# A second MLP layer with stationary weights in a fused convolution and windowed-attention kernel, and one convolution matmul moved forward

## The chip, the core and the metric

The kernel runs as one program on one core of a Trainium2 chip. The metric is device time in microseconds (us), the median of several runs; lower is better. The core has five instruction streams that run side by side and meet at semaphores: TensorE (PE, matmuls; its weight loads are shown as PEld), VectorE (DVE), ScalarE (ACT), GpSimd (POOL) and SyncE (SP), which here issues all the DMAs. A strip of the work passes between them many times, so what counts is the longest chain through all of them.

## The reference

The input x is 32 images of 56 x 56 pixels with 128 channels, float32. Two layers follow each other.

```python
# layer 0: ResNeXt block (convolutions without bias, _bn = affine with fixed statistics)
h = relu(_bn(conv1x1(x, w1), ...))             # 128 -> 64 channels
h = relu(_bn(conv3x3(h, w2, groups=32), ...))  # 64 -> 64
h = _bn(conv1x1(h, w3), ...)                   # 64 -> 128
x = relu(h + x)
# layer 1: shifted-window attention block, windows of 7 x 7, 8 heads of 16
y   = roll(_ln(x, norm1_w, norm1_b), (-3, -3))
q, k, v = windows(y) @ qkv_w.T
attn = softmax(q @ k.T * scale + bias + mask)
x = x + roll(windows_back(attn @ v @ proj_w.T + proj_b), (3, 3))
z = _ln(x, norm2_w, norm2_b)
z = gelu(z @ fc1_w.T + fc1_b) @ fc2_w.T + fc2_b   # 128 -> 512 -> 128
return x + z
```

The change touches `@ fc2_w.T`, the second MLP layer, and the order of work in layer 0.

## The kernel before

There are two stages, one behind the other. All matmuls are float32.

**The convolution stage** goes over 16 pairs of images, the loop body holding two pairs and the last pairs being written out. An image pair is cut into 8 chunks of 7 rows. A pair is done in two steps of four chunks (`STEPS` = 2, `GROUPS` = 4). In a step, PE does conv2, the 3 x 3 convolution (line 517, 144 matmuls into banks 0 to 3), and conv3 in two halves of 32 matmuls (line 530), one for each image of the pair, again into banks 0 to 3. Between these, it already makes conv1 (line 497) for four chunks of the next pair: `x_to_channels` (line 488) turns a chunk of x so that channels lie on partitions, DVE copies it into the tile xct (`xct_out`, line 918), conv1 multiplies, and ACT writes the result to the tile h1 (`h1_out`, line 748). There is one xct buffer for each of the two images. `conv1(gp, i)` needs the copy of chunk i; `x_to_channels` for chunk i+1 comes right behind it in the function `produce`. The second half of conv3 may write the banks only when DVE has added the first half's results to x (`sum_out`, line 931). conv2 of the next step waits for the sums of the second half; conv2 of the next pair also waits for all eight h1 chunks. ACT finishes a chunk with a relu (`relu_out`, line 764), and SP stores it. Each engine runs its own list in the order in which its function `period` writes it; nothing is reordered across engines but by semaphores. On DVE the order in a step is: copies of chunks 1 and 2, the four sums of half 0, the copy of chunk 3, the four sums of half 1, the copy of the next chunk 0.

**The attention stage** goes over 256 strips, eight per image, each strip a row of 8 windows (392 pixels, `ST`), held as 4 pairs of windows of 98 pixels (`PAIRS`, `PT`). It is software-pipelined over strips: in one turn of `strips(t)`, PE does queries, keys, values and scores of strip t, the attention of strip t-1, and the MLP of strip t-3. DVE makes the layer norms, adds the bias to the scores and takes the maxima; POOL subtracts them; ACT does the exponentials, the Gelu and the copies out of PSUM. The order on each engine is again that of its `strips` function. The MLP of a strip uses one PSUM bank, `RC`, by turns (`C_JOBS` = 4 turns: z transposed, two of the four hidden chunks, the output), with the semaphores c_full and c_out; the other two hidden chunks go through bank `RA`. `mlp_out(t, p)` makes the MLP's output with pixels on partitions: for window pair p, four matmuls (line 659), one for each 128 hidden channels. The stationary operand is the 98-pixel piece of g, the moving one is fc2, 128 columns wide. That is 16 matmuls for each strip; two pairs stand ahead of `attend(t1, 1)` and two behind the transposes of the next strip's xn. DVE then adds the residual (`y_sum`, line 1039), and SP stores.

Other lines that the steps name: 582 `project` (queries, then keys), 567 transposes of xn and z, 575 values, 651 hidden layer, 592 scores, 605 transposes of the probabilities, 628 row sums, 617 `attend`, 638 output projection; on ACT 793 `xt_out`, 798 `q_out`, 823 `pt_out`, 829 and 832 `reciprocals`, 860 the load of the table for exponentials, 837 the exponentials; on DVE 1012 the norms, 1000 `ot_out` (the attention output times the reciprocal, which the projection reads).

Of the kernel before, what the change touches and what calls it, by code (L numbers as in the profile page):

```python
# [142 lines left out]
def program(nc, a, out):  # L143
# [6 lines left out]
    with ctx:  # L150
        def sb(name, shape, dtype=fp32):
            return ctx.enter_context(nc.sbuf_tensor(name, shape, dtype))
# [77 lines left out]
        z = sb("z", [PT, PAIRS, C])  # L230
        zt = sb("zt", [C, ST])
        g = sb("g", [128, HC, ST])
        y = sb("y", [PT, 2, PAIRS, C])

        bank = [ctx.enter_context(nc.psum_tensor(f"bank{i}", [128, 512], fp32)) for i in range(8)]
# [3 lines left out]
        B_JOBS = (4, 5)  # L239
        SUMS, PROJECTION = 3, 4  # L240
        SMALL = 6
        C_JOBS = 4


        conv_load, bias_load, wload, prep, tb_store, tb_load = sem("conv_load"), sem("bias_load"), sem("wload"), sem("prep"), sem("tb_store"), sem("tb_load")
# [218 lines left out]
        def _(pe):  # L464
# [33 lines left out]
                                          start=True, stop=True)  # L498
                mm.then_inc(conv1_ps, 1)

            def produce(gp, u, i):
                conv1(gp, i)
                if i + 1 < CHUNKS:
                    x_to_channels(gp, u, i + 1)
                elif later(gp, 1):
                    x_to_channels(gp + 1, 1 - u, 0)

            def conv2(gp, u, s):
                pe.wait_ge(h1_sb, CHUNKS * (gp + 1))
# [36 lines left out]
            def period(gp, u):  # L546
                for s in range(STEPS):
                    conv2(gp, u, s)
                    if later(gp, 1):
                        produce(gp + 1, 1 - u, GROUPS * s)  # L550
                        produce(gp + 1, 1 - u, GROUPS * s + 1)
                    conv3(gp, s, 0)
                    if later(gp, 1):
                        produce(gp + 1, 1 - u, GROUPS * s + 2)
                    conv3(gp, s, 1)
                    if later(gp, 1):
                        produce(gp + 1, 1 - u, GROUPS * s + 3)

            over_pairs(pe, fill, period)
            pe.wait_ge(prep, len(PREP))  # L560
# [90 lines left out]
                nc.tensor.matmul(ring[:, 0:ST], fc1[:, 128 * j:128 * j + 128], zt[:],  # L651
                                 start=True, stop=True).then_inc(full, 1)

            def mlp_out(t, p):

                pe.wait_ge(c_out, C_JOBS * t.n + 3)
                pe.wait_ge(hidden_out, 2 * t.n + 2)
                for c in range(HC):
                    mm = nc.tensor.matmul(RC[0:PT, C * p:C * p + C], g[:, c, PT * p:PT * p + PT], fc2[:, c, :],  # L659
                                          start=c == 0, stop=c == HC - 1)  # L660
                if p == PAIRS - 1:
                    mm.then_inc(c_full, 1)

            def strips(t):
                ahead, t1, t2, t3 = t.back(-1), t.back(1), t.back(2), t.back(3)
                if t.there():
                    pe.wait_ge(a_out, A_JOBS * t.n + 1)
                    project(t, 0)
                if t3.there():
                    pe.wait_ge(z_sb, t3.n + 1)  # L670
                    wait(pe, c_out, C_JOBS * t3.n)
                    to_channels(RC, z, c_full)
                if t.there():
                    values(t, 0)
                    project(t, 1)
                    values(t, 1)
                if t3.there():
                    hidden(t3, 0)
                if t.there():
                    scores(t, 0)  # L680
                if t3.there():
                    hidden(t3, 1)
                if t.there():
                    scores(t, 1)
                if t3.there():
                    hidden(t3, 2)
                if t1.there():
                    probs_t(t1, 0)
                    probs_t(t1, 1)
                if t3.there():  # L690
                    hidden(t3, 3)
                if t1.there():
                    probs_t(t1, 2)
                    probs_t(t1, 3)
                if t1.there():
                    row_sums(t1)
                    attend(t1, 0)
                if t3.there():
                    mlp_out(t3, 0)
                    mlp_out(t3, 1)  # L700
                if t1.there():
                    attend(t1, 1)
                if ahead.there():
                    pe.wait_ge(xn_sb, ahead.n + 1)
                    wait(pe, a_out, A_JOBS * ahead.n)
                    if t3.there():
                        pe.wait_ge(hidden_out, 2 * t3.n + 2)
                    to_channels(RA, xn, a_full)
                if t3.there():
                    mlp_out(t3, 2)  # L710
                    mlp_out(t3, 3)
                if t1.there():
                    projection(t1)

# [3 lines left out]
        def _(act):  # L718
# [54 lines left out]
            def period(gp, u):  # L773
                for s in range(STEPS):
                    h2_out(gp, s)
                    if later(gp, 1):
                        h1_out(gp + 1, 1 - u, GROUPS * s)
                        h1_out(gp + 1, 1 - u, GROUPS * s + 1)
                    relu_out(gp, u, s, 0)
                    if later(gp, 1):  # L780
                        h1_out(gp + 1, 1 - u, GROUPS * s + 2)
                    relu_out(gp, u, s, 1)
                    if later(gp, 1):
                        h1_out(gp + 1, 1 - u, GROUPS * s + 3)

            over_pairs(act, fill, period)
            for c in range(CHUNKS):
# [25 lines left out]
            def gelu(t, j):  # L813
                ring, full, out_, n = ((RC, c_full, c_out, C_JOBS * t.n + 2 + j // 2) if j % 2 == 0 else
                                       (RA, hidden_full, hidden_out, 2 * t.n + 1 + j // 2))
                act.wait_ge(full, n)
                nc.scalar.activation(g[:, j], ring[:, 0:ST], ACT.Gelu, bias=fc1b[:, j:j + 1]).then_inc(out_, 1)  # L817

            def pt_out(t, j):
                act.wait_ge(b_full[j % 2], b_before(t, j % 2, 1 + j // 2) + 1)  # L820
# [18 lines left out]
            def strips(t):  # L839
                ahead, t1, t2, t3 = t.back(-1), t.back(1), t.back(2), t.back(3)  # L840
                if t.there():
                    q_out(t)
                if t3.there():
                    zt_out(t3)
                if t.there():
                    k_out(t)
                if t3.there():
                    gelu(t3, 0)
                    gelu(t3, 1)
                    gelu(t3, 2)  # L850
                if t1.there():
                    pt_out(t1, 0)
                    pt_out(t1, 1)
                if t3.there():
                    gelu(t3, 3)
                if t1.there():
                    pt_out(t1, 2)
                    pt_out(t1, 3)
                if t.there() or t1.there():
                    nc.scalar.preload_act_table_set("natural_log_exp_and_others")  # L860
                if t.there():
                    exponentials(t, 0)
                if t1.there():
                    reciprocals(t1)
                if ahead.there():
                    xt_out(ahead)
                if t.there():
                    exponentials(t, 1)
# [10 lines left out]
        def _(dve):  # L879
# [153 lines left out]
                norm_stats(1, t, x2)  # L1033

            def y_sum(t):
                dve.wait_ge(c_full, C_JOBS * t.n + 4)
                wait(dve, y_out[t.u], 16 * MOVES * t.half)
                dve.wait_ge(res2_sb, t.n + 1)
                V.tensor_tensor(out=y[:, t.u].rearrange("p k c -> p (k c)"), in0=RC[0:PT, :],
# [180 lines left out]
```

## Time and profile before

| | |
|---|---|
| median of 3 runs (lowest, highest) | 5296.85 us (5293.0, 5299.09) |
| the profiled execution's own time | 5297.13 us |
| its span, first to last instruction | 5295.3 us |
| busy: PE, PEld, DVE, ACT, POOL | 91%, 69%, 69%, 64%, 50% |
| mean granted TensorE clock | 0.98 |
| second MLP layer's matmuls, line 659 | 8192 records, 998.6 us busy |

The busy shares are averages over the two stages. In the profile's 40 slices PE is at 8 tenths in the convolution stage and at 9 (90% or more) in every slice of the attention stage but the last. A float32 matmul that is not a transpose leaves two records, a transpose one; "x32" on line 659 therefore means 16 matmuls. A line's busy time counts the drain of the last matmul, which overlaps the next instruction's start; from start to start the times are a little shorter.

### The profile page before, as it was taken

The numbers are of one execution on the slowest core, as the hardware profiler recorded it, in microseconds if no ns is written. First come the engines' busy times: TensorE is split into PE (matmuls) and PEld (weight loads), VectorE is DVE, ScalarE is ACT, GpSimd is POOL, SyncE is SP. The second block draws the span as 40 slices with busy tenths as digits, with TensorE's granted clock in tenths as the row PEclk, the third lists the DMA queues.
The fourth block names the chain that finished last, engine by engine and source line by source line (L and its number), as shares of the span: only waits on it lengthen the run. The fifth ranks groups of instructions, "written<-read, shape, count | busy, mean of one in ns | idle before, by whom it ended". The sixth has DMA issues, their size and how long they took to land.

```text
span 5295.3 us, 197343 instructions
## 1 busy us (share of the span) xinstructions
PE 4843.6 (91%) x73224; PEld 3669.2 (69%) x73224; DVE 3643.9 (69%) x7453; ACT 3405.9 (64%) x5387; POOL 2623.6 (50%) x3763
## 2 busy tenths in 40 slices
PE   3688888599999999999999999999999999999998
PEld 1455566477777777777777777777777777777776
DVE  2233333577777777777777777777777777777775
ACT  1233333377777777777777777777777777777776
POOL 6233333355555555555555555555555555555554
PEclk7899999799999999999999999999999999999999
DMA  2344443100000000000000000000000000000000
GB/s 63 103 130 129 133 130 117 34 26 25 26 26 26 26 26 26 26 25 25 26 26 25 25 26 26 26 26 25 25 25 26 26 26 26 26 26 26 26 25 22
DMA packets 304837, 219.26 MB, mean 41 GB/s; under 512 B 49206, under 2 KB 252008, under 8 KB 304680
## 3 DMA queue, kind: packets, MB, share of 16 engines
q1 hardware_dynamic: 304680, 216.83, 14.0%
q8 instruction: 140, 2.29, 0.2%
q14 instruction: 17, 0.14, 0.0%
HBM read 111.15 MB, written 111.94 MB: 42 GB/s over the span
## 4 chain that ended last, share of the span: by engine, by line
PE 70%; DVE 15%; issue 8%; ACT 3%; SPq 2%; DVEq 1%; POOL 1%; DMA 0%; ACTq 0%; POOLq 0%
PE bank L659 13%; PE bank L651 11%; PE bank L575 9%; DVE xn L1012 8%; PE bank L582 7%; PE bank L592 5%; PE bank L517 5%; PE bank L638 4%; PE bank L567 4%; DVE sc L987 4%; PE bank L530 4%; ACT shared L823 2%; PE bank L605 2%; PE bank L628 2%; PE bank L617 2%
## 5 line engine op out<-in xcount | busy, mean ns | idle before, releaser
L659 PE MATMUL bank<-fc_sb,g 128*98 128x128 f32 x8192 | 998.6, 275 | 1.5 <-ACT g L817 1.5
L659 PEld LDWEIGHTS bank<-fc_sb,g 128*98 128x98 f32 x8192 | 910.2, 165 | 19.8 <-ACT g L817 2.7
L651 PE MATMUL bank<-zt,fc_sb 128*128 128x392 f32 x2048 | 895.0, 519 | 3.0 <-ACT zt L810 2.3
L1153 POOL TENSOR_TENSOR res<-x,projb 98x512 f32<-98x512 f32 x256 | 325.4, 1271 | 1122.2 <-DVE x L1029 1122.2
L1012 DVE TENSOR_SCALAR xn<-x,lnp 98x128 f32<-98x128 f32 x1024 | 838.1, 879 | 4.0 <-POOL lnp L1082 4.0
L1171 POOL TENSOR_TENSOR sc<-sc,mx 128x784 f32<-128x784 f32 x512 | 775.5, 1517 | 11.2 <-DVE mx L993 3.3
L987 DVE TENSOR_TENSOR sc<-bank,shared 128x392 f32<-128x392 f32 x1024 | 528.8, 558 | 324.5 <-PE bank L592 324.4
L817 ACT ACTIVATE g<-bank,fc1b 128x392 f32<-128x392 f32 x1024 | 586.7, 587 | 247.8 <-PE bank L651 244.5
L605 PEld LDWEIGHTS bank<-ident_sb,sc 128*98 128x98 f32 x4096 | 465.2, 127 | 174.7 <-issue 98.1
L1082 POOL TENSOR_TENSOR lnp<-st 98x8 f32<-98x8 f32 x777 | 144.9, 214 | 847.9 <-DVE st L875 847.9
L971 DVE TENSOR_TENSOR shared<-bank,vmask_sb 98x512 f32<-98x512 f32 x512 | 354.0, 691 | 283.0 <-PE bank L575 283.0
L575 PEld LDWEIGHTS bank<-wqkv,xt 128*98 128x98 f32 x4096 | 486.1, 165 | 84.2 <-issue 46.8
L575 PE MATMUL bank<-wqkv,xt 128*98 128x128 f32 x4096 | 533.7, 273 | 0.0
L605 PE MATMUL bank<-ident_sb,sc 128*98 128x128 f32 x4096 | 531.0, 273 | 0.3
L993 DVE TENSOR_REDUCE mx<-sc 128x16 f32<-128x784 f32 x512 | 496.6, 970 | 18.4
L1082 POOL TENSOR_TENSOR lnp<-lnp,half 98x8 f32<-98x8 f32 x518 | 478.7, 924 | 30.3 <-POOL lnp L1082 19.8
L875 DVE BATCH_NORM_STATS2 st<-x 98x6 f32<-98x128 f32 x2048 | 442.9, 278 | 36.4 <-DMA x_scratch<-shared 3.7
L823 ACT ACTIVATE shared<-bank 98x392 f32<-98x392 f32 x1024 | 453.0, 493 | 4.4 <-PE bank L605 4.4
L837 ACT ACTIVATE sc<-sc 128x784 f32<-128x784 f32 x512 | 435.8, 851 | 15.3 <-POOL sc L1171 12.5
L793 ACT ACTIVATE xt<-bank,ln 128x784 f32<-128x784 f32 x256 | 257.0, 1004 | 291.6 <-PE bank L567 291.6
L582 PE MATMUL bank<-xt,wqkv 128*128 128x392 f32 x1024 | 432.0, 503 | 2.5 <-ACT xt L793 2.5
L918 DVE COPY xct<-bank 128x392 f32<-128x392 f32 x256 | 133.0, 559 | 410.7 <-PE bank L488 410.5
(87 smaller groups left out, 7698.9 us busy)
## 6 DMA issues: line engine op xcount, KB each, us to landing
x<-x_scratch SPq DMA_DIRECT2D x768, 49.0 KB
out_x<-y SPq DMA_DIRECT2D x672, 49.0 KB
xc_even<-in_x SPq DMA_DIRECT2D x128, 196.0 KB
shared<-in_x SPq DMA_DIRECT2D x128, 196.0 KB
x_scratch<-xc_even SPq DMA_DIRECT2D x128, 196.0 KB
x_scratch<-shared SPq DMA_DIRECT2D x128, 196.0 KB
x<-x_scratch SPq DMA_DIRECT2D x256, 38.5 KB
out_x<-y SPq DMA_DIRECT2D x224, 38.5 KB
```

The source lines that it names most:

```text
L575: mm = nc.tensor.matmul(RB[j][0:PT, C * w:C * w + C], rows, wqkv[:, 2 * C:3 * C], start=True, stop=True)
L582: nc.tensor.matmul(RA[:, 0:ST], wqkv[:, C * i:C * i + C], xt[:, :, 0, :], start=True, stop=True).then_inc(a_full, 1)
L605: mm = nc.tensor.transpose(RB[j % 2][0:PT, 128 * q:128 * q + 128], sc[:, t.u, q, j].rearrange("p h m -> p (h m)"), ident[:])
L651: nc.tensor.matmul(ring[:, 0:ST], fc1[:, 128 * j:128 * j + 128], zt[:], start=True, stop=True).then_inc(full, 1)
L659: mm = nc.tensor.matmul(RC[0:PT, C * p:C * p + C], g[:, c, PT * p:PT * p + PT], fc2[:, c, :], start=c == 0, stop=c == HC - 1)
L817: nc.scalar.activation(g[:, j], ring[:, 0:ST], ACT.Gelu, bias=fc1b[:, j:j + 1]).then_inc(out_, 1)
L823: nc.scalar.activation(pt[:, j], full_[:, :, :, 0:N], ACT.Copy).then_inc(b_out[j % 2], 1)
L987: V.tensor_tensor(out=sc[:, t.u, q].rearrange("p k h m -> p (k h m)"), in0=bank[q][:, 0:ST], in1=b.rearrange("p k h m -> p (k h m)"), op=A ...
L993: V.reduce_max(mx[:, r].rearrange("p q k h -> p (q k h)"), sc[:, t.u, 2 * r:2 * r + 2].rearrange("p q k h m -> p (q k h) m"), AX.X).then_i ...
L1012: ins = V.tensor_scalar(dst[:, p, :], src[:, p, :], lnp[:, 8, i, p:p + 1], lnp[:, 9, i, p:p + 1], ALU.mult, ALU.add)
L1082: return P.tensor_tensor(out=o, in0=x, in1=y_, op=op)
L1171: P.tensor_tensor(out=s_r, in0=s_r, in1=m_r.to_broadcast([128, 2 * HEADS, N]), op=ALU.subtract).then_inc(sub_done, 1)
```

## The change

The second MLP layer is computed the other way round: the stationary operand is now a 128 x 128 piece of fc2, the moving one is g with all 392 pixels of the strip. So four matmuls of 392 columns make the output with channels on partitions. ACT copies it from PSUM to a new tile yt (`yt_out`), and PE turns it back in four transposes (`mlp_to_tokens`). RC now has five turns for each strip. The first two of the four matmuls need only the first two hidden chunks and stand ahead of `row_sums`. In the convolution stage conv1 of a step's last chunk stands ahead of the second half of conv3, while `x_to_channels` stays behind it; on ACT the last h1_out of the step stands ahead of both relu_out blocks.

```diff
-        C_JOBS = 4
+        C_JOBS = 5
...
                     conv3(gp, s, 0)
                     if later(gp, 1):
                         produce(gp + 1, 1 - u, GROUPS * s + 2)
+                        conv1(gp + 1, GROUPS * s + 3)
                     conv3(gp, s, 1)
                     if later(gp, 1):
-                        produce(gp + 1, 1 - u, GROUPS * s + 3)
+                        next_x_to_channels(gp + 1, 1 - u, GROUPS * s + 3)
...
-            def mlp_out(t, p):
+            def mlp_out(t, r):
 
                 pe.wait_ge(c_out, C_JOBS * t.n + 3)
-                pe.wait_ge(hidden_out, 2 * t.n + 2)
-                for c in range(HC):
-                    mm = nc.tensor.matmul(RC[0:PT, C * p:C * p + C], g[:, c, PT * p:PT * p + PT], fc2[:, c, :],
-                                          start=c == 0, stop=c == HC - 1)
-                if p == PAIRS - 1:
+                pe.wait_ge(hidden_out, 2 * t.n + r + 1)
+                for c in (2 * r, 2 * r + 1):
+                    mm = nc.tensor.matmul(RC[:, 0:ST], fc2[:, c, :], g[:, c], start=c == 0, stop=c == HC - 1)
+                if r == 1:
                     mm.then_inc(c_full, 1)
+
+            def mlp_to_tokens(t):
+                pe.wait_ge(c_out, C_JOBS * t.n + 4)
+                for p in range(PAIRS):
+                    mm = nc.tensor.transpose(RC[0:PT, C * p:C * p + C], yt[:, PT * p:PT * p + PT], ident[:])
+                mm.then_inc(c_full, 1)
...
+                if t3.there():
+                    mlp_out(t3, 0)
                 if t1.there():
                     row_sums(t1)
                     attend(t1, 0)
                 if t3.there():
-                    mlp_out(t3, 0)
                     mlp_out(t3, 1)
...
                     to_channels(RA, xn, a_full)
                 if t3.there():
-                    mlp_out(t3, 2)
-                    mlp_out(t3, 3)
+                    mlp_to_tokens(t3)
...
-                    relu_out(gp, u, s, 0)
                     if later(gp, 1):
                         h1_out(gp + 1, 1 - u, GROUPS * s + 2)
+                        h1_out(gp + 1, 1 - u, GROUPS * s + 3)
+                    relu_out(gp, u, s, 0)
                     relu_out(gp, u, s, 1)
-                    if later(gp, 1):
-                        h1_out(gp + 1, 1 - u, GROUPS * s + 3)
...
+            def yt_out(t):
+                act.wait_ge(c_full, C_JOBS * t.n + 4)
+                nc.scalar.activation(yt[:], RC[:, 0:ST], ACT.Copy).then_inc(c_out, 1)
...
                 if t1.there():
                     reciprocals(t1)
+                if t3.there():
+                    yt_out(t3)
                 if ahead.there():
                     xt_out(ahead)
```

PE's order in the second half of a strip's turn, from the last hidden chunk to the next strip's queries, before:

```order
L651 MATMUL bank<-zt,fc_sb 128x392
L605 MATMUL bank<-ident_sb,sc 98x128 x8
L628 MATMUL bank<-shared,vmask_sb 32x392 x4
L617 MATMUL bank<-shared 32x49 x16
L659 MATMUL bank<-fc_sb,g 98x128 x8
L617 MATMUL bank<-shared 32x49 x16
L567 MATMUL bank<-ident_sb,xn 128x98 x4
L659 MATMUL bank<-fc_sb,g 98x128 x8
L638 MATMUL bank<-wproj,ot 98x128 x4
```

The same place now:

```order
L656 MATMUL bank<-zt,fc_sb 128x392
L610 MATMUL bank<-ident_sb,sc 98x128 x8
L664 MATMUL bank<-g,fc_sb 128x392 x2
L633 MATMUL bank<-shared,vmask_sb 32x392 x4
L622 MATMUL bank<-shared 32x49 x16
L664 MATMUL bank<-g,fc_sb 128x392 x2
L622 MATMUL bank<-shared 32x49 x16
L572 MATMUL bank<-ident_sb,xn 128x98 x4
L671 MATMUL bank<-ident_sb,yt 98x128 x4
L643 MATMUL bank<-wproj,ot 98x128 x4
```

Two wide matmuls (line 664) now stand between the transposes of the probabilities and the row sums, and four transposes (line 671) stand between those of xn and the projection, where eight matmuls were.

PE's order in the convolution stage, from the first half of conv3 to the end of the step, with what each row waits for, before (line 497 is conv1, 488 are the transposes of x):

```order
L530 MATMUL bank<-w_sb,h 98x128 x31
L496 REGISTER_ALU [waits h1_sb]
L497 MATMUL bank<-xct,w_sb 64x392 [waits xct_sb0]
L497 MATMUL bank<-xct,w_sb 64x392 [waits xct_sb1]
L488 MATMUL bank<-ident_sb,shared 128x98 [waits xct_sb0,xc_in16]
L488 MATMUL bank<-ident_sb,shared 128x98 x3
L488 MATMUL bank<-ident_sb,shared 128x98 [waits xct_sb1]
L488 MATMUL bank<-ident_sb,shared 128x98 x3
L526 REGISTER_ALU [waits h2_sb]
L530 MATMUL bank<-w_sb,h 98x128 [waits xc_summed]
L530 MATMUL bank<-w_sb,h 98x128 x31
L496 REGISTER_ALU [waits h1_sb]
```

And now, from the transposes of the same chunk on:

```order
L489 MATMUL bank<-ident_sb,shared 128x98 [waits xct_sb0,xc_in16]
L489 MATMUL bank<-ident_sb,shared 128x98 x3
L489 MATMUL bank<-ident_sb,shared 128x98 [waits xct_sb1]
L489 MATMUL bank<-ident_sb,shared 128x98 x3
L497 REGISTER_ALU [waits h1_sb]
L498 MATMUL bank<-xct,w_sb 64x392 [waits xct_sb0]
L498 MATMUL bank<-xct,w_sb 64x392 [waits xct_sb1]
L530 REGISTER_ALU [waits h2_sb]
L534 MATMUL bank<-w_sb,h 98x128 [waits xc_summed]
L534 MATMUL bank<-w_sb,h 98x128 x31
```

conv1 of the last chunk (498), with its waits for the two copies into xct, now comes ahead of the wait for the sums (534). DVE's order has not changed.

ACT's order around the new copy (line 830), at the end of a strip's turn (850 exponentials, 842 and 845 reciprocals, 802 xt_out):

```order
L850 ACTIVATE sc<-sc 128x784 [waits sub_done]
L842 ACTIVATE logsum<-bank 128x392 [waits b_full1]
L845 ACTIVATE rsum<-logsum 128x392 [waits b_out0,b_out1]
L830 ACTIVATE yt<-bank 128x392 [waits c_full]
L802 ACTIVATE xt<-bank,ln 128x784 [waits a_full]
L850 ACTIVATE sc<-sc 128x784 [waits sub_done]
```

The copy waits for line 664's last matmul, and behind it in the queue stands xt_out, which the next strip's queries need. No table load stands beside it.

## Rows read from the trace of the kernel before

**Rows 1.** Windows view, the attention stage: busy (count) of PE, PEld, DVE, ACT, POOL; clock.
```profile
1190.00:5300.00 4110.00, 3934.79 (x55841) 3033.54 (x55839) 3180.60 (x6597) 2960.03 (x4657) 2156.32 (x3437) 1.00 0.09 25
```

**Rows 2.** Chain of waits, two strips: start us, us, what.
```profile
3003.74 0.68 PE bank L582 x2
...
3017.31 0.56 PE bank L567 x4
3017.86 1.75 PE bank L659 x16
...
3020.49 0.67 PE bank L582 x2
...
3037.07 0.67 PE bank L582 x2
```

**Rows 3.** Timeline, PE, attention: start, us, line, tiles, count [idle before].
```profile
3026.41 0.93 PE L651 MATMUL bank<-zt,fc_sb 128*128 128x392 f32 x2
...
3028.71 1.04 PE L605 MATMUL bank<-ident_sb,sc 128*98 128x128 f32 x8
3030.33 0.87 PE L628 MATMUL bank<-shared,vmask_sb 98*32 98x392 f32 x8 [0.59 <-ACT shared L823]
3031.01 0.53 PE L617 MATMUL bank<-shared 98*32 98x49 f32 x32
3031.48 1.99 PE L659 MATMUL bank<-fc_sb,g 128*98 128x128 f32 x16
...
5254.14 1.58 PE L651 MATMUL bank<-zt,fc_sb 128*128 128x392 f32 x4 [0.77 <-ACT zt L810]
```

**Rows 4.** Timeline, ACT, attention.
```profile
3004.45 0.51 ACT L798 ACTIVATE qt<-bank 128x392 f32<-128x392 f32 x1 [1.55 <-PE bank L582]
...
3017.90 1.00 ACT L793 ACTIVATE xt<-bank,ln 128x784 f32<-128x784 f32 x1 [1.16 <-PE bank L567]
...
3030.30 1.28 ACT L860 ACT_TABLE_LOAD   x1
...
3032.94 0.53 ACT L832 ACTIVATE rsum<-logsum 128x392 f32<-128x392 f32 x1
```

**Rows 5.** Timeline, DVE, attention.
```profile
3018.20 0.55 DVE L1000 TENSOR_TENSOR ot<-bank,rsum 128x392 f32<-128x392 f32 x1
...
3034.71 0.56 DVE L1000 TENSOR_TENSOR ot<-bank,rsum 128x392 f32<-128x392 f32 x1
```

**Rows 6.** Timeline, PE, convolution.
```profile
726.24 1.35 PE L497 MATMUL bank<-xct,w_sb 128*64 128x392 f32 x4 [0.32 <-DVE xct L918]
...
734.05 3.16 PE L530 MATMUL bank<-w_sb,h 32*98 32x128 f32 x64 [0.92 <-DVE shared L931]
...
739.86 8.16 PE L517 MATMUL bank<-h,w_sb 32*32 32x392 f32 x288 [1.01 <-DVE shared L931]
...
764.94 9.43 PE L517 MATMUL bank<-h,w_sb 32*32 32x392 f32 x288 [2.35 <-ACT h L748]
...
198.19 1.56 PE L488 MATMUL bank<-ident_sb,xc_even 98*128 98x98 f32 x8 [35.26 <-DMA xc_even<-in_x]
```

**Rows 7.** Timeline, DVE, convolution.
```profile
725.62 1.04 DVE L918 COPY xct<-bank 128x392 f32<-128x392 f32 x2 [12.38 <-PE bank L488]
...
731.52 2.48 DVE L931 TENSOR_TENSOR shared<-bank,shared 98x512 f32<-98x512 f32 x4 [2.37 <-PE bank L530]
733.92 1.03 DVE L918 COPY xct<-bank 128x392 f32<-128x392 f32 x2
...
760.97 2.48 DVE L931 TENSOR_TENSOR shared<-bank,shared 98x512 f32<-98x512 f32 x4 [2.29 <-PE bank L530]
```

**Rows 8.** Timeline, ACT, convolution.
```profile
764.03 0.66 ACT L748 ACTIVATE h<-bank,bn 128x392 f32<-128x392 f32 x1
```

**Rows 9.** Windows view, start of two conv2 blocks; the number behind POOL is the clock.
```profile
713.80:717.00 3.20, 3.20 (x75) 1.72 (x84) 0.00 (x0) 0.00 (x0) 0.06 (x1) 0.50 0.86 245
740.00:748.00 8.00, 8.00 (x290) 4.70 (x283) 0.66 (x2) 0.95 (x2) 1.29 (x1) 1.00 0.82 252
```

More of the change, by code:

```diff
@@ L232, in program @@
         g = sb("g", [128, HC, ST])
+        yt = sb("yt", [C, ST])
         y = sb("y", [PT, 2, PAIRS, C])
@@ L499, in conv1, with next_x_to_channels @@
                 mm.then_inc(conv1_ps, 1)
-            def produce(gp, u, i):
-                conv1(gp, i)
+            def next_x_to_channels(gp, u, i):
                 if i + 1 < CHUNKS:
@@ L506, in produce @@
                     x_to_channels(gp + 1, 1 - u, 0)
+            def produce(gp, u, i):
+                conv1(gp, i)
+                next_x_to_channels(gp, u, i)
             def conv2(gp, u, s):
@@ L1035, in y_sum @@
             def y_sum(t):
-                dve.wait_ge(c_full, C_JOBS * t.n + 4)
+                dve.wait_ge(c_full, C_JOBS * t.n + 5)
                 wait(dve, y_out[t.u], 16 * MOVES * t.half)
```

## Prediction

> **What bounds the kernel now.** I read the windows view first: in the attention stage PE is busy for 3934.79 of 4110 us at full clock, and no other engine is near that (DVE 3180.60) [rows 1]. That says PE, but a busy share hides a loop through another engine, so the chain of waits came next. In it the queries of three strips in a row start at 3003.74, 3020.49 and 3037.07 [rows 2]: 16.75 and 16.58 us, a mean of 16.665 us for each strip. I count every time within a strip from that start and call it P. The chain runs through PE, except that in the first of the two strips it goes through DVE up to the transposes of xn at 3017.31. So DVE's norms are nearly as late as PE there. Then the timelines, for how late each engine is. PE idles once in a strip, 0.59 us ahead of the row sums, waiting for ACT's copies of the probabilities [rows 3]. DVE has ot ready at 3018.75 and 3035.27 [rows 5], that is P+15.01 and P+14.78, mean P+14.90, while PE comes to the projection only at P+15.87 (3017.86 + 1.75 = 3019.61, less 3003.74) [rows 2]. That is DVE's slack: about 1 us. Whatever PE saves beyond it is lost to the wait for ot.
>
> In the convolution stage PE is bound by turns by itself and by its waits: 0.92 us for the sums ahead of conv3's second half, 1.01 us for the sums ahead of a conv2, and 2.35 us for h1 ahead of the conv2 that opens the next pair [rows 6].
>
> **The attention stage, part by part.** Removed: 16 matmuls of 128 columns. Eight take 1.75 us in the chain [rows 2], so 3.50 us. Added: four matmuls of 392 columns. The queries are the same form (128 x 128 stationary, 392 columns moving) and take 0.67 to 0.68 us [rows 2]; four take 2.68. Added: four transposes of 98 x 128 from float32. Eight of them take 1.04 us [rows 3], so four 0.52. PE's work falls by only 0.30 us. The place matters more: the first two new matmuls, 1.34 us, stand where PE idles for 0.59 us, so that idle goes too.
>
> PE's new path, from P: the last transposes of probabilities end 0.59 us ahead of 3030.33, at 3029.74, which is P+9.25. Add the first pair of new matmuls 1.34, the row sums 0.68 and attend 0.47 (starts at 3030.33, 3031.01, 3031.48 [rows 3]), the second pair 1.34 and 0.2 for the change of shape behind attend (the old eight took 1.99 there [rows 3] against 1.75 elsewhere), so P+13.28; the other attend 0.47 and the transposes of xn 0.56 [rows 2], so P+14.31; the new transposes 0.52: P+14.83. On this path xn is needed at P+13.75; it was ready for the chain at 3017.31, P+13.57, so it still hides.
>
> Now ot. Its own chain (queries, values, scores, then DVE's sums and maxima, the norms, ot) starts at P and nothing in it has moved, so it still ends at P+14.90. Its other input, the reciprocals, ended at 3033.47 [rows 4], P+12.98; the row sums now end at P+11.27, and ACT reads them after P+11.8, so they hide. So ot is late next, by 0.07 us over PE's path. The projection then starts at P+14.94 (0.04 for the handover, as from 3017.86 to 3017.90 [rows 2, 4]) and takes 0.88 (3019.61 to 3020.49), and the next strip starts at P+15.82. Gain: 16.665 - 15.82 = 0.845 us. It holds for the strips in which all parts are present, 252 of 256: 213 us. The last strips stay as they are, since their wide matmuls save about what the copy costs.
>
> The added waits. The copy to yt can start at P+13.28; a copy of this form takes 0.51 [rows 4], with two handovers it is there at P+13.87, and PE asks for it at P+14.31: hidden by 0.44. Behind it in ACT's queue stands xt_out, which starts when the xn transposes end, P+14.35, takes 1.00 [rows 4] and ends at P+15.35; the next queries want it at P+15.82: hidden by 0.47. If either cover went, each 0.1 us would cost 25 us in all. What xt_out pushes back is the copy of the queries, and ACT idles 1.55 us ahead of that [rows 4]. y_sum on DVE starts behind ot in both orders.
>
> Bounds. The new matmuls with back-to-back weights: two of the hidden layer's take 1.58 us together, drain included [rows 3]; by that the path is 0.48 longer, P+15.31, and the strip 16.19. Below, PE cannot gain anything: ot holds the strip at 15.82. I take 1.34, because a weight load hides behind 392 columns in the queries, and because only two of the four stand behind another shape.
>
> **The convolution stage.** On DVE the copy of chunk 3 stands behind the four sums of half 0, and that did not change. The sums run from 731.52 to 734.00 and the copy starts at 733.92 [rows 7]. conv1 of that chunk used to come later than the copy by itself. Now it stands ahead of conv3's second half and waits for the copy. The row that shows this wait is conv1 at 726.24: the copy had started at 725.62, and conv1, which gets its two operands one after the other, ended at 727.59, 1.97 after the copy's start [rows 6, 7]. So conv3's second half starts at 733.92 + 1.97 = 735.89 in place of 734.05: 1.84 late. The sums of half 1 and the next conv2, which waits for them (739.86 [rows 6]), move by the same; the 0.8 us of conv1 saved behind conv3 only lengthens the wait there. At a pair's end conv2 waited for h1, which ACT wrote behind its relus (764.03 to 764.69 [rows 8]); now h1 is early, and the sums are last: 760.97 + 2.48 + 1.84 + 0.1 = 765.39 against 764.94, 0.45 late. Together 2.29 us for a pair of images. 15 pairs make conv1 for a next one, but in the first of them PE waits 35.26 us for a load behind it [rows 6], which hides it: 14 x 2.29 = 32 us lost.
>
> The unknown here is PE's clock. It fell to the lower of its two levels, 1.2 GHz (0.50 in the windows view [rows 9]), at the conv2 behind the wait of 2.35 us, in 11 of 14 pairs, and never behind the wait of 1.01 us. A fall costs 9.43 - 8.16 = 1.27 us [rows 6]. The waits ahead of the two conv2 are now about 2.0 us each (1.01 + 1.84 - 0.8, and 765.39 less the end of PE's earlier work), between the two cases. No fall at all would give back 11 x 1.27 = 14 us, a fall at each of 28 would cost 22 more. I take no change: 32.
>
> **A rule that speaks against it.** The Trainium skill, page "TensorE: Matmul & The Clock Gate", section on the PE-mode transpose, says that a transpose does not count as PE work for the clock gate in the same way as a matmul. Transposes of x stand directly ahead of each wait. By that rule the stretches without counted work are those 0.8 us longer, and one more of them appears, ahead of the moved conv1. The trace of before fits both readings, since the transposes stand ahead of the long and of the short wait alike.
>
> **The sum.** -213 + 32 = -181 us on the profiled execution's 5297.1 us (span 5295.3), which equals the median of 5296.85: 5116 us.
>
> **Rivals.**
> - The clock falls more: also at the two conv2 of a pair and at the moved conv1, which now waits about 1.5 us. All 56 places would cost (56 - 11) x 1.27 = 57 us more, 5173; at half of that, 5145. For it: 2.35 us was enough 11 times. Against: 1.01 us never was. Chance 0.15.
> - The weight loads of the new matmuls are not hidden. A single hidden matmul behind another shape took 0.93 us [rows 3], 0.86 without the drain. Four times 0.19 over 0.67, less the 0.2 already counted, lengthens PE's path by 0.56 to P+15.39 and the strip to 16.27: 252 x 0.395 = 100 us gained, less 32: 5229. For it: float32 weights of 128 columns behind a 32-row shape. Against: the queries' 0.67. Chance 0.07.
> - Slower: the copy to yt asks for another function table in ACT, between the logarithm and the exponential. Then there are two more loads of 1.28 us [rows 4] in a strip, one ahead of the copy and one behind it. The copy ends at 12.98 + 1.28 + 0.51 = P+14.77, xt_out runs from P+16.05 to P+17.05, and the strip takes 17.1: 252 x 0.43 = 108 lost, and 32, so 5437. It decides from 1.2 us of delay of xt_out on, where the strip's gain falls below the 32 / 252 = 0.13 us of the convolution. Against: the copies to pt and qt are of this kind and run under either table, and no load is listed beside line 830. Chance 0.02.
> - The moved conv1 does what it seems meant to do, filling the wait ahead of conv3's second half: then nothing is lost and the pair's end gains up to 1.4 us: 5297 - 213 - 19 = 5065. Against: DVE's order. Chance 0.01.
>
> **How the numbers follow.** The forecast, with the clock's falls between none and 28, has a chance of 0.75 (5100 to 5140). The rivals have 0.15, 0.07, 0.02 and 0.01. The range for 8 in 10 takes in the first rival almost whole and ot's own spread (P+14.78 to P+15.01, 29 us each way at most): 5085 to 5170. A change under 0.2%, 11 us, can't be told from none with this kernel's runs. Faster by more: 0.96; within: 0.01; slower: 0.03.
>
> **What would show it.** In the attention stage of the new profile: a strip of 15.8 us from queries to queries; no wait ahead of the row sums; two rows of about 1.34 us for the new matmuls; a short or no wait of the projection, put down to ot; none for xt ahead of the queries; and no idle of the new transposes for yt. In the convolution: conv1 of the fourth chunk waiting about 1.5 us for the copy, conv3's second half starting some 1.8 us later behind the sums, and pairs of images that take 2.3 us longer, with the clock's falls counted at each conv2. I am wrong if the projection waits for nothing and the strip is still over 16 us (weights), if the queries wait for xt (ACT), or if the convolution stage ends earlier than before.

## The result, and the profile after

The changed kernel takes 5230.19 us (median of 4 runs, 5227.38 to 5238.73) against 5297.02 us before: a ratio of 0.9879 with a 95% interval of 0.9863 to 0.9895, or 67 us less. I had forecast 5116 us, 181 less, with a range up to 5170. The direction is right; the size is far off, and the time lies outside the range.

The windows view of the attention stage after the change (busy and count of PE, PEld, DVE, ACT, POOL; clock) answers to [rows 1]:

```profile
1190.00:5150.00 3960.00, 3845.86 (x50751) 2588.00 (x50742) 3154.14 (x6589) 3069.42 (x4880) 2151.16 (x3417) 1.00 0.10 26
```

PE is as busy as before, 97% of the stretch against 96%, though 5,120 of its 73,224 matmul records are gone, and the shares alone would say that nothing but PE matters. The page's summary of the chain that ended last says otherwise:

```profile
PE 48%; DVE 34%; issue 12%; SPq 2%; DVEq 2%; POOL 1%; ACT 0%; DMA 0%; ACTq 0%; POOLq 0%
```

Before, DVE had 15% of that chain; now it has 34%. The chain's pieces at the end of two strips (start us, us, what) show where it crosses from DVE to PE, and answer to [rows 2]:

```profile
3011.19 0.49 DVE ot L1015
3011.68 0.12 issue
3011.80 1.11 PE bank L643 x8
3012.91 0.67 PE bank L587 x2
...
3027.39 0.48 DVE ot L1015
...
3027.99 1.11 PE bank L643 x8
3029.11 0.67 PE bank L587 x2
```

The queries start at 3012.91 and 3029.11, so this strip takes 16.20 us; over 36 strips the mean is 16.233, where I had 15.82 and before it was 16.665. In each strip ot ends the DVE part, then the projection runs, then the queries. The timeline of PE for the same strip (start us, us, line, tiles, count, [idle before]) answers to [rows 3]:

```profile
3012.74 0.84 PE L587 MATMUL bank<-xt,wqkv 128*128 128x392 f32 x2
...
3022.00 1.48 PE L664 MATMUL bank<-g,fc_sb 128*128 128x392 f32 x4
3023.42 0.87 PE L633 MATMUL bank<-shared,vmask_sb 98*32 98x392 f32 x8
...
3024.56 1.58 PE L664 MATMUL bank<-g,fc_sb 128*128 128x392 f32 x4
...
3026.57 0.56 PE L572 MATMUL bank<-ident_sb,xn 98*128 98x98 f32 x4
3026.96 0.60 PE L671 MATMUL bank<-ident_sb,yt 128*98 128x128 f32 x4
3027.99 1.11 PE L643 MATMUL bank<-wproj,ot 128*98 128x128 f32 x8 [0.43 <-DVE ot L1015]
3028.94 0.84 PE L587 MATMUL bank<-xt,wqkv 128*128 128x392 f32 x2
```

The idle ahead of the row sums is gone: line 633 follows the first pair of new matmuls at once. There is a new idle of 0.43 us ahead of the projection, put down to ot. The timelines of ACT and DVE answer to [rows 4] and [rows 5]:

```profile
3025.37 0.53 ACT L845 ACTIVATE rsum<-logsum 128x392 f32<-128x392 f32 x1
3026.18 0.50 ACT L830 ACTIVATE yt<-bank 128x392 f32<-128x392 f32 x1 [0.29 <-PE bank L664]
3027.16 1.00 ACT L802 ACTIVATE xt<-bank,ln 128x784 f32<-128x784 f32 x1 [0.48 <-PE bank L572]
...
3029.82 0.51 ACT L807 ACTIVATE qt<-bank 128x392 f32<-128x392 f32 x1 [0.91 <-PE bank L587]
```

```profile
3027.31 0.55 DVE L1015 TENSOR_TENSOR ot<-bank,rsum 128x392 f32<-128x392 f32 x1
...
3029.14 0.69 DVE L1044 TENSOR_TENSOR x<-bank,res 98x512 f32<-98x512 f32 x1 [0.68 <-PE bank L643]
```

The copy to yt (line 830) ends at 3026.68 and is asked for at 3026.96; x^T (line 802) ends at 3028.16, and the queries start at 3028.94. Both covers held. ot ends at 3027.86, and the projection starts at 3027.99.

In the convolution stage, PE's and DVE's timelines answer to [rows 6] and [rows 7] (498 is conv1, 534 conv3, 489 the transposes, 521 conv2; 946 the sums, 933 the copy):

```profile
736.52 0.89 PE L489 MATMUL bank<-ident_sb,shared 98*128 98x98 f32 x8
738.81 1.34 PE L498 MATMUL bank<-xct,w_sb 128*64 128x392 f32 x4 [1.40 <-DVE xct L933]
740.09 3.16 PE L534 MATMUL bank<-w_sb,h 32*98 32x128 f32 x64
743.18 0.89 PE L489 MATMUL bank<-ident_sb,xc_even 98*128 98x98 f32 x8
745.89 9.28 PE L521 MATMUL bank<-h,w_sb 32*32 32x392 f32 x288 [1.82 <-DVE xc_even L946]
```

```profile
735.80 2.48 DVE L946 TENSOR_TENSOR xc_even<-bank,xc_even 98x512 f32<-98x512 f32 x4 [2.37 <-PE bank L534]
738.20 1.03 DVE L933 COPY xct<-bank 128x392 f32<-128x392 f32 x2
```

conv1 of the fourth chunk waits 1.40 us for the copy at 738.20, which stands behind the four sums; conv3's second half follows at 740.09, and conv2 waits 1.82 us. The queries of the first strip start at 979.9 us before and at 1023.9 us after, so the convolution stage is 44 us longer. The clock at the start of that conv2, as [rows 9]:

```profile
745.50:748.50 3.00, 2.61 (x65) 1.27 (x66) 1.19 (x3) 0.91 (x2) 1.02 (x1) 0.50 0.75 248
```

It is at 1.2 GHz again. Of the first 28 conv2 blocks behind 215 us, the granted clock shows the lower level within the first 3 us of 24; before, it was 11. All counts of falls below are made in this way. In the changed kernel, PE waits 2.5 to 3 us ahead of seven of the 28, six of them at the loop's start, and the clock fell at all seven; of the other 21, with 1.8 us of idling ahead, it fell at 17.

### The profile page after: what moved, and what is told of

Its sections match the earlier page's. It is cut to its first block, busy times and chain, and to the rows that moved or that the text cites. A ratio compares the mean times of both kernels' runs of the same rounds, so it can differ in the third digit from the quotient of the medians.

```text
span 5228.0 us, 187347 instructions
## 1 busy us (share of the span) xinstructions
PE 4803.1 (92%) x68104; PEld 3244.2 (62%) x68104; DVE 3623.3 (69%) x7453; ACT 3531.7 (68%) x5643; POOL 2626.9 (50%) x3763
## 4 chain that ended last, share of the span: by engine, by line
PE 48%; DVE 34%; issue 12%; SPq 2%; DVEq 2%; POOL 1%; ACT 0%; DMA 0%; ACTq 0%; POOLq 0%
DVE xn L1027 16%; PE bank L580 9%; DVE sc L1002 8%; PE bank L656 7%; PE bank L587 7%; PE bank L597 6%; PE bank L643 5%; PE bank L521 5%; DVE z L1027 4%; PE bank L534 4%; DVE ot L1015 2%; PE bank L498 2%; PE bank L572 2%; SPq L381 1%; DVE shared L946 1%
## 5 line engine op out<-in xcount | busy, mean ns | idle before, releaser
L664 PE MATMUL bank<-g,fc_sb 128*128 128x392 f32 x2048 | 784.6, 506 | 0.0
L664 PEld LDWEIGHTS bank<-g,fc_sb 128*128 128x128 f32 x2048 | 348.1, 190 | 161.2 <-ACT g L826 1.2
L813 ACT ACTIVATE km<-bank,headmask_sb 128x392 f32<-128x392 f32 x512 | 273.9, 587 | 214.3 <-PE bank L587 214.3
```

The lines of the kernel that those rows point to most:

```text
L664: mm = nc.tensor.matmul(RC[:, 0:ST], fc2[:, c, :], g[:, c], start=c == 0, stop=c == HC - 1)
```

## The experiments

All times are medians. A ratio to the kernel before is to runs of it that were taken beside the experiment, in three sets (medians 5291.8, 5296.5 and 5291.7 us). Times within a strip are counted from the start of the queries in PE's timeline, as means of 35 strips or more between 2000 and 2600 us. In the convolution stage I split every step into three: from conv2's start to conv3's first half, to its second half, to the next conv2; means of 24 steps from 215 us on.

### The two parts of the change, each alone

```diff
# conv_only: before, plus
                         produce(gp + 1, 1 - u, GROUPS * s + 2)
+                        conv1(gp + 1, GROUPS * s + 3)
                     conv3(gp, s, 1)
-                        produce(gp + 1, 1 - u, GROUPS * s + 3)
+                        next_x_to_channels(gp + 1, 1 - u, GROUPS * s + 3)
# (and ACT's h1_out of chunk 3 ahead of both relu_out); mlp_only: after, with these lines undone
```

> The kernel before with only the convolution stage's part of the change (conv1 of a step's last chunk ahead of conv3's second half, ACT's h1_out ahead of the relus). Theory A, the two parts add up and the convolution costs what the first queries' start shows (979.9 us before, 1023.9 after): about 5297 + 44 = 5341 us, with a half-clock stretch at some 23 of 28 conv2 blocks. Theory B, my forecast's price without more clock falls: 5329 us. Theory C, the convolution part is harmless by itself and the MLP part's gain was simply smaller: 5297 us.

> The changed kernel with the convolution stage's order put back. Theory A: about 5230 - 44 = 5186 us, strips of 16.23 us as in the changed kernel, convolution as before (first queries at about 980 us). Theory B: 5198. Theory C: 5230, no difference.

Measured: conv_only 5339.76, 48 us more (ratio 1.0097, 1.008 to 1.0114). mlp_only 5178.61, 113 us less (0.9788, 0.9772 to 0.9804). The sum, 65 less, is the changed kernel's 67. So theory A holds and C falls: the parts are independent. The convolution part is not harmless, and the MLP part alone is 100 us short of my 213. The strip of mlp_only takes 16.237 us.

### What holds the strip: ot on DVE, or PE's own work

```diff
# mlp_ot: mlp_only, DVE's order; before_ot: the same edit on the kernel before
+                if t1.there():
+                    ot_out(t1)
                 if t2.there():
                     x2_norm(t2)
-                if t1.there():
-                    ot_out(t1)
# mlp_late: mlp_only, PE's order; mlp_late_ot: both edits
-                if t3.there():
-                    mlp_out(t3, 0)
                 if t1.there():
                     row_sums(t1)
                     attend(t1, 0)
                 if t3.there():
+                    mlp_out(t3, 0)
                     mlp_out(t3, 1)
```

> mlp_only, and on DVE ot_out stands ahead of the four norms of z (x2_norm) in place of behind them. Theory 1, the strip is held by ot: ot comes about 1 us earlier, the projection's wait goes, PE is the bound again; PE's path gives 15.5 to 15.6 us for a strip in place of 16.23, so 160 to 180 us less than mlp_only, about 5015 us. Theory 2, the gain fell short because the new matmuls load their weights in the open and PE's own work fills the strip: no difference from mlp_only, about 5186 us. Theory 3, the norms of z moved behind ot become the late ones (transposes of z in the next strip wait): 5100 or more.

Measured: 5032.59 us, 0.9516 of before (0.95 to 0.9532), 146 less than mlp_only, where I expected 160 to 180, from moving four norms behind one instruction. The strip takes 15.639 us, where I expected 15.5 to 15.6. PE's and DVE's timelines of mlp_ot at the end of a strip (670 the new transposes, 642 the projection, 586 the queries; 1015 ot, 1027 the norms of z):

```profile
3030.20 0.60 PE L670 MATMUL bank<-ident_sb,yt 128*98 128x128 f32 x4
3030.64 1.11 PE L642 MATMUL bank<-wproj,ot 128*98 128x128 f32 x8
3031.59 0.87 PE L586 MATMUL bank<-xt,wqkv 128*128 128x392 f32 x2
```

```profile
3029.94 0.57 DVE L1015 TENSOR_TENSOR ot<-bank,rsum 128x392 f32<-128x392 f32 x1 [0.51 <-PE bank L621]
3030.43 1.11 DVE L1027 TENSOR_SCALAR z<-x,lnp 98x128 f32<-98x128 f32 x4
```

The projection starts 0.44 us behind the new transposes' start, with no idle. Theory 1 holds but for the size; theories 2 and 3 fall. One thing in these rows matters later: ot ends at 3030.51, only 0.13 us ahead of the projection, the same distance as where the projection waited for it. ot now starts as soon as PE's second attend (line 621) lets it. So PE's own work and the way through ot end together in this kernel, and ot has no slack left.

> mlp_only, with the first pair of new matmuls put back behind the row sums and the first attend, so that PE's idle of 0.59 us ahead of the row sums returns. Theory 1 (ot holds the strip, PE has half a microsecond of slack): the path of PE grows by 0.6 and comes out at about 16.3 us a strip, only 0.05 to 0.15 over mlp_only: 5200 to 5225 us. Theory 2 (PE's own work holds the strip): 0.59 more for each of 252 strips, about 5186 + 149 = 5335 us.

> mlp_ot with the first pair of new matmuls back behind the row sums, so both PE's idle of 0.59 us and the early ot. Theory 1 (longest of two paths): PE's path alone decides and is that of mlp_late, 16.3 us a strip: 5198 us, so early ot is worth nothing here and the place of the pair is worth 165 us. Theory 2 (gains add up): mlp_late less 146 us, 5052.

> The kernel before with only DVE's order changed: ot_out ahead of the norms of z. Theory 1 (before, PE holds the strip and ot has about 0.7 us of slack): no difference, within 10 us of 5292 to 5297. Theory 2 (ot early is worth something by itself, whatever the MLP does): the 146 us that it was worth in mlp_ot, or a good part, 5150 to 5250.

Measured: mlp_late 5198.52, only 20 more than mlp_only, though PE's idle is back in each strip. mlp_late_ot 5202.69, so the change of DVE's order is worth nothing here. before_ot 5292.84 (ratio 0.9996, 0.9986 to 1.0005): nothing. PE's timeline of mlp_late:

```profile
3002.70 0.87 PE L632 MATMUL bank<-shared,vmask_sb 98*32 98x392 f32 x8 [0.59 <-ACT shared L835]
...
3003.85 2.90 PE L663 MATMUL bank<-g,fc_sb 128*128 128x392 f32 x8
3006.68 0.56 PE L621 MATMUL bank<-shared 98*32 98x49 f32 x32
3007.17 0.56 PE L571 MATMUL bank<-ident_sb,xn 98*128 98x98 f32 x4
3007.57 0.60 PE L670 MATMUL bank<-ident_sb,yt 128*98 128x128 f32 x4
3008.01 1.11 PE L642 MATMUL bank<-wproj,ot 128*98 128x128 f32 x8
```

It idles 0.59 us ahead of the row sums (632) as before, the transposes of xn come 0.7 us later than in mlp_only, and the projection follows without a wait. DVE's rows for ot, first in mlp_late and then in mlp_late_ot:

```profile
3007.32 0.56 DVE L1014 TENSOR_TENSOR ot<-bank,rsum 128x392 f32<-128x392 f32 x1
```

```profile
3006.69 0.57 DVE L1014 TENSOR_TENSOR ot<-bank,rsum 128x392 f32<-128x392 f32 x1 [0.94 <-PE bank L621]
```

In mlp_late_ot, DVE idles 0.94 us until PE's second attend. In mlp_late the four norms of z fill that time. ot therefore starts at 14.65 us of the strip in both: the edit didn't make it earlier. In before_ot, DVE's row for ot (line 1000) and PE's for the projection (638):

```profile
3015.17 0.57 DVE L1000 TENSOR_TENSOR ot<-bank,rsum 128x392 f32<-128x392 f32 x1
```

```profile
3017.35 1.04 PE L638 MATMUL bank<-wproj,ot 128*98 128x128 f32 x8
```

ot is ready at 3015.74 and the projection comes at 3017.35, since PE holds that strip. The four kernels with the new matmuls show what holds the strip. With the late pair, it takes 16.293 or 16.295 us in either order of DVE, because PE's attend comes late and ot waits for it; with the early pair 16.237, and with early ot too 15.639. The place of the first pair is worth 0.06 us as long as ot is late, and 0.66 us once it isn't.

### The convolution stage: the copy, h1 and the clock

```diff
# conv_copy_mid: conv_only, DVE's order
-                    sum_out(gp, u, s, 0)
+                    sum_out(gp, u, s, 0, range(2))
                         next_xct_out(gp + 1, GROUPS * s + 2)
+                    sum_out(gp, u, s, 0, range(2, GROUPS))
# before_h1: before, ACT's order (also on mlp_ot, as mlp_ot_h1)
                         h1_out(gp + 1, 1 - u, GROUPS * s + 2)
+                        h1_out(gp + 1, 1 - u, GROUPS * s + 3)
                     relu_out(gp, u, s, 1)
-                        h1_out(gp + 1, 1 - u, GROUPS * s + 3)
```

> conv_only, and on DVE the copy of a step's last chunk stands between the second and the third sum of half 0. Theory D (the moved conv1 waits for this copy, which stood behind all four sums): conv1 starts about 1.3 us earlier, and the second half of conv3 now waits for the last sum, which the copy pushed back by 1.0 us: from conv3's first to its second half 7.1 us in place of 7.47, about 10 us less than conv_only, 5330. Theory F (conv1 there costs its own length, whatever the copy does): 7.47 as before, 5340.

Measured: 5316.09, 24 less than conv_only. conv3's halves are 6.79 us apart in place of 7.47 (5.72 before). Its rows for the moved conv1 (497) and conv3's second half (533):

```profile
745.77 1.34 PE L497 MATMUL bank<-xct,w_sb 128*64 128x392 f32 x4 [0.32 <-DVE xct L921]
747.44 3.16 PE L533 MATMUL bank<-w_sb,h 32*98 32x128 f32 x64 [0.32 <-DVE shared L934]
```

conv1 now waits 0.32 us and conv3 0.32 us for the sums. Theory D holds. The gain is larger than I expected: the first image's transposes were ready when the second sum ended, so the copy followed at once, 0.3 us earlier than I had put it, and the clock fell at 18 of 28 conv2 blocks, against 26 in conv_only.

> The kernel before, with only ACT's order changed: both h1_out of a step's second half stand behind the first relu_out and ahead of the second. PE and DVE keep their order. Theory D (the conv2 that opens a pair waits for h1 because that copy stands behind the relus, and the loss in the changed kernel comes from PE's conv1 waiting for DVE's copy): that conv2 starts with the sums, 1.3 us earlier in 14 or 15 pairs, so 19 us less, and some more if the clock falls less often behind the shorter wait; 5265 to 5280 us. Theory E (the late h1 only moves the wait): no difference, 5295 us.

> mlp_ot with the same change of ACT's order. If the two parts are independent: mlp_ot's 5033 less what before_h1 gains, 5005 to 5015 us. If the gain in the convolution stage is given back at the passage to the attention stage (SP's stores and loads): 5033.

Measured: before_h1 5266.23, 25 less (0.9956, 0.9942 to 0.9969); mlp_ot_h1 5007.37, again 25 less than mlp_ot, and 0.9463 of before (0.945 to 0.9476). It is the fastest version. In before_h1, the row of a conv2 that opens a pair and what stands ahead of it (530 conv3, 497 conv1, 488 transposes):

```profile
756.18 3.16 PE L530 MATMUL bank<-w_sb,h 32*98 32x128 f32 x64 [0.92 <-DVE xc_even L930]
759.27 0.88 PE L497 MATMUL bank<-xct,w_sb 128*64 128x392 f32 x4
760.08 0.89 PE L488 MATMUL bank<-ident_sb,shared 98*128 98x98 f32 x8
761.99 7.72 PE L517 MATMUL bank<-h,w_sb 32*32 32x392 f32 x271 [1.02 <-DVE xc_even L930]
```

The wait is 1.02 us, for the sums, where it was 2.35 for h1 [rows 6]. So an early h1 is the useful half of the convolution part. That PE's order is the harmful one follows by comparison: conv_only also has the early h1 and is 48 us slower than before, where before_h1 is 25 faster. The comparison isn't quite clean, since before_h1 keeps the first relu_out ahead of the two h1_out, and no run has PE's order without ACT's. There was no fall of the clock at any of the first 28 conv2 blocks, and the part from conv2 to conv3 takes 12.79 us in place of 13.44.

```diff
# fill_t: after, transposes ahead of conv2 made three times
-                    for t in range(TILES):
+                    for t in TILES_THRICE if i % GROUPS == 0 and conv_begun else range(TILES):
# fill_m: after, a matmul ahead of the transposes of each image
+                    if i % GROUPS == 0 and conv_begun:
+                        nc.tensor.matmul(bank[4 + m][:, 0:CHT], ident[:], h2[:, m], start=True, stop=True)
```

> The changed kernel with the eight transposes of x behind conv3's second half made three times over, into the same bank, which fills 1.6 of the 1.82 us in which PE waits ahead of conv2; the output stays. Theory T (transposes keep the clock no more than idling does): the clock still falls at some 23 of 28 conv2 blocks, and the time stays at about 5230. Theory I (PE's idling decides): with 0.2 us of idle no fall, 23 x 1.3 = 30 us less, 5200.

> The changed kernel with two matmuls of 128 x 128 by 392 columns (1.34 us, their result is overwritten, the output stays) ahead of those eight transposes, which fills 1.3 of the 1.82 us. Theory T and theory I both: matmuls hold the clock, no or few falls at conv2, about 30 us less than the changed kernel, 5200. If the falls stay, then neither idling nor transposes are what brings the clock down there, and the time stays at 5230.

Measured: fill_t 5236.14, fill_m 5219.47 us. The clock fell at 6 and at 1 of 28 conv2 blocks, against 24 in the changed kernel. Two rows of PE in fill_t (492 the tripled transposes), and the clock behind them:

```profile
752.54 2.24 PE L492 MATMUL bank<-ident_sb,xc_even 98*128 98x98 f32 x24
755.26 5.23 PE L525 MATMUL bank<-h,w_sb 32*32 32x392 f32 x184 [0.48 <-DVE xc_even L950]
```

```profile
755.26:758.50 3.24, 3.24 (x133) 2.23 (x134) 0.80 (x2) 0.52 (x1) 1.96 (x1) 1.00 0.75 240
```

conv2 opens at the upper level behind 2.24 us of nothing but transposes and 0.48 us of idling. It did so at all 21 places where the transposes filled the wait down to 0.5 us, of which 17 fell in the changed kernel. The 6 falls that are left came at the other seven places, where PE still waits 2.5 to 3.6 us. So the transposes held the clock, as the matmuls of fill_m did, and it was PE's idling that let it fall. Theory T falls for the clock, and with it, in this kernel, the rule on the PE-mode transpose (the Trainium skill, page "TensorE: Matmul & The Clock Gate", section on the PE-mode transpose) that I had weighed; the measurement decides. Whether transposes alone would raise the clock, no run shows. Nor is the idling directly ahead of conv2 all that counts: in fill_m it is 1.4 to 1.9 us at six places, behind its two matmuls, and none of them fell.

The times didn't follow, however. fill_m gained 11 us where I expected 30, and fill_t none. The steps show where it went. The part from conv2 to conv3 takes 13.44 us in fill_m and 13.73 in fill_t (changed kernel 13.83). Without falls, PE waits more inside the conv2 blocks, 0.65 and 0.80 us a block against 0.32. The profile puts that to "issue", which is time for which it shows no releaser; that the instructions come late is my reading, and no run took this apart. And in one step of four, the loop's start, the added work did not fill a wait but came on top: there the part from conv3's second half to conv2 takes 8.4 us in fill_t and 7.1 in fill_m, against 6.7. In fill_t this alone is some 12 us, more than the falls gave back.

## Why the prediction was wrong

**The sum of the strip, -213 us: measured -113.** This is the step that failed. The mechanism was as I put it: PE's idle gone, ot late next, both new copies covered. The term that was mis-sized is the way from ot to the next queries, "the next strip starts at P+15.82": it measured 16.233, and since the strip was now bound there, each error counted 252 times. The rows of the kernel before that I had not read are PE's timeline of the projection and the queries, and DVE's of the norms of xn:

```profile
3019.45 1.04 PE L638 MATMUL bank<-wproj,ot 128*98 128x128 f32 x8
3020.32 0.84 PE L582 MATMUL bank<-xt,wqkv 128*128 128x392 f32 x2
```

```profile
3013.98 3.27 DVE L1012 TENSOR_SCALAR xn<-x,lnp 98x128 f32<-98x128 f32 x4
```

- **Two clocks mixed: 0.17 us.** The chain view has these queries at 3020.49 [rows 2], the timeline at 3020.32. Behind other PE work, the chain puts a piece's start at the end of the piece ahead of it, with the drain. I counted ot from the chain's P, compared it with the projection's start in the chain, and then added 0.88 for the projection from a true start, which gives the next strip's start in the timeline, not in the chain. In one view, ot ended at 15.06 and the projection came at 15.79: the slack was 0.73 us, not "about 1".
- **The handover from DVE to PE: 0.09.** ot's end to the projection's start is 0.13 us (3027.86 to 3027.99). I had used 0.04, the handover from PE to ACT. A row of the same two engines would not have helped: the norms of xn end at 3017.25, and their transposes start at 3017.31 [rows 2], 0.06 later. ot to the projection is 0.13 in every strip in which it waits; why that place takes twice as long is open.
- **The projection: 0.07.** From its start to the queries' start it takes 0.95 us against 0.87 before. All the kernels with the new matmuls have 0.95, before_ot has 0.87 like before. Two things differ between these groups, and no run parts them: the projection stands behind the new transposes, and ot ends only 0.13 us ahead of it (0.7 us or more in the others). mlp_ot, where ot starts earlier, doesn't settle it, since the projection does too and the 0.13 us between them stays. Which of the two costs the 0.07 is open.
- **ot itself: 0.09.** It ends at 15.15 in place of 15.06 us from the queries in the timeline. The first bias addition on DVE already starts 0.09 later. Why is open.

Together 0.42 us, where the strip missed my forecast by 0.413, and that times 252 is 104 us of the 114 that I was off; the convolution's 12 to 16 us are the rest, to within a few us.

**PE's path.** I had PE ready for the projection at P+14.83 and ot 0.07 us behind it. P+14.83 is 15.00 in the timeline's count, and there PE is ready at 14.65 (the new transposes start at 14.215 and take 0.44): 0.35 us too much, because I had added up busy times with their drains, at the transposes of the probabilities and of xn above all. So the closeness of the two paths was an artefact. ot ends 0.50 us behind PE's path, and the projection starts at 15.285, 0.6 us behind it, which is what mlp_ot won back. My range's bounds hung on PE's path, where I expected the surprise; ot, the floor, I had taken as exact.

**The hidden copies, 0.44 and 0.47 us of cover.** Right: 0.28 and 0.78 in the rows above, and no wait.

**conv1 behind the copy, +1.84 us a step.** Right: 1.74 us between conv3's halves (7.46 against 5.72), and conv_copy_mid showed the cause.

**The pair's end, h1 early.** Right: the wait went from 2.35 to 1.82 us, near the 2.0 that I had. At the loop's start, one of four steps, conv2 comes 0.85 us later than in the others, mostly put down to issue; before, the wait for h1 covered this, and I didn't foresee it.

**The clock, "I take no change".** Wrong: falls went from 11 to 24 of 28. The part from conv2 to conv3 grew by 0.39 us a step, and the part from conv3's second half to conv2 shrank by 0.46. Together, 28 steps x (1.74 - 0.46 + 0.39) = 47 us, where I had 32 and conv_only measured 48. A fall isn't worth the 1.27 us that I took: fill_m has 23 fewer and gains 11 us.

**The rivals.** Table loads, weights in the open and a filled wait did not come. The rival of weights in the open had 5229 us, and the kernel took 5230: that is chance. It had PE's path holding the strip and no wait of the projection. The projection waits, PE's four new matmuls take 1.42 and 1.52 us a pair from start to start (I had 1.34 and 1.54), and mlp_ot, with the same matmuls, is 146 us faster than mlp_only. The rival of more falls did come in part, and by fill_t it was PE's idling that brought them, not the transposes.

## What to carry to other kernels

When a wait is taken away, the gain ends at the next-latest input, and then the handover from that input counts in full. Count its slack in one view, from its end to the start of what needs it, and give the handover a range: between DVE and PE it was 0.06 us at one place and 0.13 at another. Before moving work into a PE wait, look at what the moved work itself waits for in the other engines' lists; here, DVE's order had to change with PE's (0.60 us a strip in mlp_ot), and conv1 had its copy on the wrong side of the sums. A change of order on the engine that feeds the bound (146 us in mlp_ot) can be worth more than the new form of the matmuls (93 us in mlp_late, where they fill no idle). An edit that moves an instruction forward in its queue need not make it start earlier: look at what it waits for, as with ot in mlp_late_ot.

## What I had not expected of the hardware

Transposes kept TensorE at 2.4 GHz as matmuls did: with 1.8 us of idling ahead of conv2 it fell to 1.2 GHz at 17 of 21 places, and with the same stretch filled with transposes, 0.5 us of idling left, at none of them. And a lower clock cost less than its length says: fill_m, with 23 fewer falls, gains 0.39 us in the part from conv2 to conv3, where a fall alone had cost 1.27 [rows 6]; a part of the rest is that PE waits 0.33 us more inside each conv2 block.
